# Graph attention on one core: third tile's masks ahead of the plus tables, x by rows in two halves, paired stores, and three of eight products on GpSimd

## The reference

```python
in_fts = W @ inlayer.T
f1 = (w1 @ in_fts).T + b1
f2 = (w2 @ in_fts).T + b2
logits = f1 + f2.T
bias_mat = jnp.where(adj_mat > 0, 0.0, NEG_INF).astype(logits.dtype)
coefs = jax.nn.softmax(jax.nn.leaky_relu(logits) + bias_mat, axis=-1)
vals = coefs @ inlayer
...
x = _layernorm(x + _L0_gnn_ref(x, adj, ...), axis=-1)
```

## Time and profile before

| | us |
|---|---|
| median of 3 runs | 278.81 (277.19 to 279.4) |
| profiled execution | 275.19 |
| its span | 273.5 |
| PE busy | 258.2 (94%) |
| DVE busy | 242.6 (89%) |
| ACT busy | 195.6 (72%) |
| POOL busy | 67.2 (25%) |
| PE clock granted (mean share of full speed) | 0.997 |
| DMA, mean over the span | 269 GB/s, 73.64 MB |

### The profile page before, as it was taken

One profiled execution on the slowest core, in us unless ns is written; L12 is line 12 of the kernel. 1 busy time (PEld: TensorE's weight loads), 2 busy tenths in 40 slices (PEclk: granted clock), 3 DMA queues, 4 the chain that ended last, 5 costly groups with the idle time before them and its releaser, 6 DMA issues.

```text
span 273.5 us, 5997 instructions
## 1 busy us (share of the span) xinstructions
PE 258.2 (94%) x2195; PEld 225.6 (82%) x2195; DVE 242.6 (89%) x309; ACT 195.6 (72%) x296; POOL 67.2 (25%) x98
## 2 busy tenths in 40 slices
PE   2999988799999999999999999999999999999991
PEld 2989877688888888888888888888888888888880
DVE  2888999988888899999999999999998999999963
ACT  2479999949999996999199919991999198003140
POOL 4002046930000006300630063006300630054150
PEclk9999999999999999999999999999999999999998
DMA  6999999999999999999999999999999999801011
GB/s 196 256 298 309 311 313 282 285 272 311 313 315 318 315 314 315 323 339 315 316 324 342 318 316 280 361 328 327 240 335 309 309 285 337 226 2 38 0 49 31
DMA packets 22562, 73.64 MB, mean 269 GB/s; under 512 B 3090, under 2 KB 4244, under 8 KB 22548
## 3 DMA queue, kind: packets, MB, share of 16 engines
q1 hardware_dynamic: 11184, 35.17, 42.9%
q10 hardware_dynamic: 9956, 34.64, 42.0%
q0 software_dynamic: 1408, 3.67, 4.7%
HBM read 71.37 MB, written 2.10 MB: 269 GB/s over the span
## 4 chain that ended last, share of the span: by engine, by line
DVE 58%; PE 16%; issue 8%; ACT 7%; DMA 7%; DVEq 1%; ACTq 1%; POOL 1%; POOLq 0%
DVE mn L743 19%; PE ps L1091 16%; DVE msk L756 11%; DVE mn L748 11%; DMA nat<-in_adj 5%; DVE post L855 3%; ACT sgn L474 3%; DVE ybt L870 2%; DVE bns L875 2%; ACT bt L542 2%; DVE ntot L860 2%; DVE post L857 2%; ACT post L518 2%; DMA msk<-in_x 2%; DVE mv L879 1%
## 5 line engine op out<-in xcount | busy, mean ns | idle before, releaser
L1091 PE MATMUL ps<-bt,msk 128*128 128x258 f16 x2048 | 232.1, 274 | 3.6 <-DVE msk L756 2.7
L1091 PEld LDWEIGHTS ps<-bt,msk 128*128 128x128 fp8e5 x2048 | 200.5, 98 | 34.2 <-issue 4.6
L474 ACT ACTIVATE sgn<-f2b,nf1l 128x1024 int8<-128x1024 f32 x128 | 136.4, 1144 | 5.2 <-POOL flag L409 4.0
L743 DVE TENSOR_SCALAR mn<-nat 128x4096 int8<-128x4096 int32 x32 | 73.1, 2284 | 5.0 <-DMA nat<-in_adj 4.6
L416 POOL TENSOR_SCALAR nmr<-mv 128x4 f32<-128x4 f32 x7 | 12.8, 1835 | 143.5 <-DVE mv L879 143.5
L756 DVE STREAM_TRANSPOSE msk<-mn 128x1024 uint32<-128x1024 uint32 x32 | 39.8, 1245 | 2.6
L748 DVE SCALAR_TENSOR_TENSOR mn<-sgn,mn 128x1024 uint32<-128x1024 uint32 x32 | 39.2, 1225 | 3.0 <-ACT sgn L474 2.0
L623 ACT ACTIVATE ybt<-ybt,nmr,rstd 128x128 f32<-128x128 f32 x28 | 11.5, 483 | 38.7 <-POOL nmr L421 38.7
L616 ACT ACTIVATE post<-ps,ac 128x258 f32<-128x258 f32 x60 | 24.8, 467 | 10.9 <-PE ps L1091 10.9
L761 DVE TENSOR_SCALAR msk<-msk 128x1024 uint32<-128x1024 uint32 x32 | 22.2, 695 | 1.0
L427 POOL DMA_DIRECT2D out<-ybt x24 | 13.7, 572 | 16.3 <-ACT ybt L623 14.9
(11 more groups left out here) (115 smaller groups left out, 105.2 us busy)
## 6 DMA issues: line engine op xcount, KB each, us to landing
nat<-in_adj SPq DMA_DIRECT2D x64, 512.0 KB, 15.1
nat<-in_adj ACTq DMA_DIRECT2D x64, 512.0 KB, 17.6
xn<-in_x POOLq DMA_DIRECT2D x4, 512.0 KB, 19.8
out<-ybt POOLq DMA_DIRECT2D x24, 64.0 KB, 6.6
msk<-in_x SPq DMA_DIRECT2D x8, 128.0 KB, 4.2
msk<-in_x ACTq DMA_DIRECT2D x8, 128.0 KB, 4.5
out<-ybt SPq DMA_DIRECT2D x4, 64.0 KB, 1.8
out<-post SPq DMA_DIRECT2D x4, 32.0 KB, 2.4
```

Of the source, the lines that this page charges most:

```text
L474: ins = act.activation(sgn[:, c, g * JA:(g + 1) * JA], f2b[:, :], ACT.Sign, bias=nf1l[:, bass.ds(G * t + g, 1)], scale=-1.0)
L743: dve.tensor_scalar(mn[:, c % 2], nat[:, c], 0, EDGE, ALU.is_gt, ALU.mult).then_inc(cast_done, 1)
L1091: ins = pe.matmul(ps[:, 2 * c + m, 0:2 * DV], mask_f[c][m][:, n // KB, n % KB, :], btv[m][:, n, :], start=(n == 0), stop=(n == NK - 1))
```

## The change

- VectorE: tile 2's cast, combination and transpose move ahead of the plus tables. Tile 1's cast moves ahead of the third minus `low_x`. `f2_rows` comes before the two small reductions of f2, the first `spread_f1` between the product and the reduction of the last chunk.
- TensorE: the `gram` matmuls come before the first edge sums; the minus sums of tiles 0, 1 and 2 come before any plus sums; plus tables are used in the order `ORDER = (1, 0, 2, 3)`.
- GpSimd multiplies chunks 2 and 3 of table 1 and chunk 1 of table 0 with `cs` (`scale_pool`): two before the denominators' columns, one after the second minus table is ready. The eight activations of ACT for chunk 3 of table 1 and those for chunk 1 of table 0 go, and DVE's `scale_x` of chunk 2 of table 1. The checks for `flag` are joined into fewer instructions, part of them earlier.
- ScalarE: more of f2's sums are taken by its accumulating copies (chunk 1 and chunk 2, four blocks each), `nf1l`'s first part is copied here, signs of tile 2 come before the second plus table, and tile 7's far halves are loaded right after the signs of tile 4.
- SyncE: the near halves of tiles 1 to 3 are issued after chunk 2 of x has landed.
- x by rows: two loads of 1 MB (`load_rows`), the first after `flag`, the second after `rows` of quad 1.
- Stores: two quads together, four DMAs of 128 KB in place of eight of 64 KB; tiles of the last quad are one DMA each.

```diff
+            def scale_pool(m, h):
+
+                pool.wait_ge(xl_in[h], 16 * A)
+                pool.wait_ge(cs_ready[m], 1)
+                return pool.tensor_tensor(ybuf[:, h], xl_chunk(h),
+                                          cs[:, m, h * CN:(h + 1) * CN, None].to_broadcast([P, CN, D]), ALU.mult)
+
+
+            for h in range(BCH // 2, BCH):
+                scale_pool(1, h).then_inc(y1_pool, 1)
...
+            pool.wait_ge(table_ready[1], 2)
+            scale_pool(0, 1).then_inc(y0_pool, 1)
...
+            def load_rows(h):
+
+                for g in range(G):
+                    pool.dma_start(xn[g * SQ:(g + 1) * SQ, h * NT // 2:(h + 1) * NT // 2, :],
+                                   x_h[h, g]).then_inc(xn_in, 16)
...
+                for turn in range(1, NQ // 2):
                     rows(2 * turn - 1, 1)
-                    store(2 * turn - 1, 1)
+                    if turn == 1:
+                        load_rows(1)
+                    store(turn - 1)
                     rows(2 * turn, 0)
...
-            for t in range(QT):
+            load_near(0, 0)
+
+            sp.wait_ge(xl_in[2], 16 * A)
+            for t in range(1, QT):
                 load_near(t, t)
...
             sp.wait_ge(tile_ready, 1)
-                for g in range(G // 2):
-                    store_last(sp, QT - 1, 1, g)
+                sp.dma_start(out_t[NT - 1], post[:, 1, 0, QT - 1, 0:D]).then_inc(last_stored, 16)
...
+            stat_max(1, 2, 4)
+            cast(2, 2, 0)
+            stat_out(1, 2, 4)
+            combine(2, 2)
+            dve.wait_ge(y0_pool, 1)
+            turn(2, 2)
```

More of the change, by code:

```diff
@@ L236, in gat_kernel @@
         last_stored = sem("last_stored")
-        out_stored = [sem(f"out_stored{i}") for i in range(2)]
+        out_stored = sem("out_stored")
         flag_ready = sem("flag_ready")
@@ L340, in _ @@
                         apart(sp)
[L341 to L344, removed]
+                        sp.dma_start(out_t[QT * q + c], ybt[:, 1, 0, :]).then_inc(g_stored, 16)
+                        sp.wait_ge(g_stored, 16 * (QT * q + c + 1))
                         apart(sp)
@@ L469, in load_far, with signs @@
                     load_part(act, t, c, a)
-            def signs(t, c, between=None):
+            def signs(t, c, between={}):
                 for g in range(G):
@@ L475, in signs @@
                                          bias=nf1l[:, bass.ds(G * t + g, 1)], scale=-1.0)
-                    if g == 1 and between:
-                        between()
+                    if g in between:
+                        between[g]()
                 ins.then_inc(sign_ready, 1)
@@ L560, in _ @@
             xT_out(3)
[L561 to L562 removed]
             act.wait_ge(f2b_ready, 1)
             act.wait_ge(nf1l_ready, 1)
[L565 removed]
+            signs(0, 0, between={1: lambda: xT_out(4)})
             load_far(3, 3)
             split_x(1, 0)
[L568 removed]
+            xT_out(5)
+            split_x(1, 1)
             act.wait_ge(nF2_ready, 1)
@@ L643, in _ @@
                 evacuate(0, 0, 2)
-                ahead(0, 3, 4)
+                ahead(0, 3, 4, True)
                 ahead(0, 3, 5)
@@ L674, in _ @@
                 normalise_last(1, 2, 1)
-                act.wait_ge(tile_ready, 1)
-                for g in range(G // 2, G):
-                    store_last(act, QT - 1, 1, g)
             with act.Else():
@@ L816, in _ @@
             turn(1, 1)
+            stat_max(1, 2, 4)
[4 more added lines that the diff above has]
+            turn(2, 2)
+            plus(0, 0)
+            low_x(0, 1)
+            plus(1, 1)
             dve.wait_ge(cs_ready[0], 1)
             scale_x(0, 2)
-            stat_max(1, 2, 4)
+            low_x(0, 0)
             scale_x(0, 3)
-            plus(0, 0)
-            low_x(0, 0)
-            plus(1, 1)
-            stat_out(1, 2, 4)
-            low_x(0, 1)
+            dve.wait_ge(y_act, 1)
+            plus(2, 2)
             low_x(0, 2)
             low_x(0, 3)
-            cast(2, 2, 0)
-            combine(2, 2)
-            dve.wait_ge(y_act, 2)
-            turn(2, 2)
-            plus(2, 2)
             cast(3, 3, 0)
@@ L1147, in _ @@
             edge_sums(2, 1)
-            for h in range(BCH):
-                plus_sums(h, [2])
+            pe.wait_ge(den_ready[0], 1)
+            pe.wait_ge(xeps_ready, 1)
+            plus_sums(ORDER[0], range(2))
+            plus_sums(ORDER[1], range(2))
+            plus_sums(ORDER[0], [2])
+            plus_sums(ORDER[1], [2])
+            plus_sums(ORDER[2], range(3))
+            plus_sums(ORDER[3], range(3))
             pe.wait_ge(gst_ready, 2)
@@ L1154, in _ @@
             edge_sums(3, 1)
-            for h in range(BCH):
+            for h in ORDER:
                 plus_sums(h, [3])
```

263 lines of the change are left out of this document (121 added, 142 removed).

## The result

| | before | after |
|---|---|---|
| median of 21 runs of each, in turns, us | 274.6 | 275.97 |
| lowest and highest, us | 273.77 to 279.4 | 274.96 to 281.23 |
| ratio after to before, 95% interval | | 1.005 (1.0028 to 1.0072) |
| profiled execution, us (its span) | 275.19 (273.5) | 275.71 (273.9) |
| PE busy / DVE busy / ACT busy / POOL busy | 258.2 / 242.6 / 195.6 / 67.2 | 258.6 / 246.2 / 192.7 / 71.9 |

The change makes the kernel 0.5% slower, 1.4 us. The forecast was 0.2% faster (278.2 against 278.81). The three runs on which its absolute numbers rested (277.19 to 279.4) lie above the 274.6 of the longer series, so the ratio is what can be compared. The loss is within the 1% that the forecast called the limit of what can be told, but it has the other sign, and its interval leaves out the forecast's 0.998.

A forecast was written before the change was run, and what follows sets the result against it. PE was bound by its latest start-up wait plus 0.112 us per remaining matmul. PE's end at 267.2 instead of 267.4 and a 0.4 us shorter tail gave -0.6 us: 278.2 against 278.81, range 274.0 to 282.0.

The forecast's parts named there:

- 0.4 us off the 6.07: Program's tail after PE's end: storing the last tile with one issue on SP makes it 0.4 us shorter.
- two places can be the latest wait now: PE's start-up: latest wait is the statistics transpose after 8 matmuls or tile 2's after 64; ends 267.15 or 267.2.
- Before it began at 21.99, waiting for DMA, so that earlier rows of tile 0 bring nothing here: Tile 0's cast on VectorE: put at 22.5, against 21.99 before, so earlier rows gain nothing.
- The walk: VectorE's start-up, row by row: statistics at 38.3, tile 2 transposed at 45.0, PE's end about 267.2 us.
- rival B: GpSimd's three products on VectorE's path are long: over 1% slower from 3.1 us each; 0.17 together with Rival C's bad case.
- Of the 7.3 us almost nothing is left: Tile 2's transpose: PE's wait ends 7.3 us earlier, but 64 fewer matmuls (7.2 us) are done by then.
- Rival A: VectorE doesn't wait for GpSimd's products: cast at 20.5, 274.2 us (-4.6); chance 0.35, counted with a short product.
- Rival C: Transfers hide the gain: if tile 1 is late for its cast, each us is lost; 0.17 together with rival B.
- Paired stores: GpSimd's output stores: half as many issues beside PE's stream, gain 0; VectorE's waits covered by its lead.
- the flag: Flag comes earlier, so signs of tile 4 no longer wait 4.0 us for it; hidden, no gain.

The follow-up runs named there:

- r0: The kernel before, run again with no edit: 274.72 us, ratio 1.0001, span 272.5.
- r1: The changed kernel with the last tile stored by four DMAs of 16 KB from two engines again: 275.62 us, ratio 1.0035 to the kernel before.
- r5b: The changed kernel with GpSimd's third product started only after the statistics reductions: 273.15 us, ratio 0.9947 to the kernel before.
- r6b: The changed kernel with 12 unread matmuls of 128 columns in TensorE's idle time before the f1 rows: 274.31 us, ratio 0.9988 to the kernel before.
- r4b: The changed kernel with the first 16 edge matmuls of tile 0 before gram again: 275.3 us, ratio 0.9995 to the kernel before.
- r2: The changed kernel with all three products moved from GpSimd to VectorE: 275.72 us, ratio 1.0045 to the kernel before.
- r10: The changed kernel without SyncE's wait for x's third chunk ahead of the near halves of tiles 1 to 3: 276.0 us, ratio 1.0045.
- r7b: The changed kernel with first 16 sums before gram, last tile in four DMAs, and third product behind the statistics: 275.2 us, ratio 1.0014.
- r11: r5b's kernel with GpSimd's second product also moved, beside tile 0's transpose: 274.33 us, ratio 0.9986 to the kernel before.
- r3: The kernel before with a single DMA of 64 KB for the last tile: 275.48 us, ratio 1.0019.

## Why the prediction was wrong

**The sum against the measurement.** Forecast -0.6, measured +1.4 (275.97 - 274.6). Profile to profile the change cost +0.52 (275.71 - 275.19): TensorE's end 0.0 (267.45 against 267.43, where the forecast said -0.2), the tail +0.4 (forecast -0.4), the time around the span +0.12 (1.81 for 1.69; forecast 0). The remaining 0.85 is the traces against their medians: before's was 0.59 above its 274.6, after's 0.26 below its 275.97.

The spans show where that is, without single traces: their median is 273.05 over r0's 12 runs of before and 274.1 over the changed kernel's 21, 1.05 us more. With 0.4 of it in the tail, an estimate from these numbers leaves 0.65 us up to TensorE's end, where the forecast had -0.2. So both terms of the sum had the wrong sign.

**The first failed step: "0.4 us off the 6.07", the tail.** It was worked from issue lengths alone: one issue in place of two. The traces show 3.3 us from VectorE's last instruction to the end for one DMA of 64 KB, and 2.9 us for four of 16 KB. The issue is shorter (0.53 us for 0.80); the landing is later. The term has the wrong sign and is 0.8 of the 2.0 us by which the forecast missed. In the traces this is plain; in the times it is indicated, not shown, since r1's interval overlaps.

**The second: the limits, in "two places can be the latest wait now".** The forecast named the statistics' transpose and tile 2's and missed a third: f1's spread. It is last in the changed kernel (34.44), and GpSimd's third product stands right ahead of it. The forecast charged that product 2.0 us, which was about right (1.7), to the statistics. What it put at nothing is TensorE's own work behind f1's spread: 4.06 us to the statistics' transpose at 38.50, which had been ready at 37.27. Nor did it price the pace. The reordering, with `gram` first, had taken away the 16 sums that kept TensorE busy in that place, and full speed came at 37.95 in place of 32.97. r5b (the hold away, -2.8 us), r6b (the idle time filled, -1.7) and r4b (the old order, -0.7, with intervals that all but touch) show it from three sides.

**The base.** "Before it began at 21.99, waiting for DMA, so that earlier rows of tile 0 bring nothing here" rested on one execution. In r0 the cast came at 21.01 without a wait and TensorE's end 1.0 us earlier. The walk was subtracted from a trace 0.6 us above its own median.

**Luck.** The walk's end was close to the trace's (267.2 for 267.4), but by errors that cancel: the statistics were ready 1.0 us before the forecast's 38.3, and TensorE reached them 1.2 us after they were ready.

**What was right.** VectorE waits for GpSimd's products: the forecast charged 2.0 us each and the rows show 3.0 for two and 1.7 for the third. The Trainium skill's rule cited there ("SBUF — State Buffer", section "SBUF: two separate sides"), that whichever engine starts first holds the shared ports for its whole instruction, fits the rows in both directions: VectorE's rows grow, and GpSimd's product takes 3.87 us when it starts behind a cast. It fits r5b's transpose too, which has one SBUF input and wasn't held; for the small instruction behind it, which was, no run shows why. The product itself is 1.90 us undisturbed, forecast 2.0, so rival B has no ground (its 3 x 1.1 - 0.6 is 2.7, not 2.8). Tile 2 was turned at 44.67 (forecast 45.0), the statistics stood at 37.3 (38.3), the pace was 0.112. "Of the 7.3 us almost nothing is left", because fewer matmuls are done at the earlier wait, is what happened. Rival A was false in its condition; r2 shows its cast time and why it would not have paid as worked out: adj lands at 20.8, and TensorE idles before f1 all the same. Rival C: r10 finds nothing, and tile 1's cast didn't wait in the changed kernel, but it waited 1.49 us for adj in r7b and 0.45 in r11. Paired stores cost a hidden 1.19 us of VectorE's wait at 153.52, the flag came at 44.65 and the 4.0 us of the earlier trace rows went, hidden too.

**What stays open.** Why the time around the span grew by 0.12 to 0.15 us: its median is 1.83 over 21 runs of the changed kernel and 1.69 over 12 of r0. It is 1.70 in r3 and 1.83 to 1.86 in r1 and r2, so it lies neither with the last store nor with GpSimd's products. GpSimd's and VectorE's loop code changed, but no run takes that apart. Why one 64 KB DMA lands later than four of 16 KB is measured and not explained.

## What to carry to other kernels

Moving element-wise work to GpSimd isn't free help for VectorE: put such an instruction beside VectorE work that takes no second input (a transpose), never ahead of the one that TensorE waits for; one wait on GpSimd turned this change from 0.5% slower to 0.5% faster. When a reordering lets TensorE idle before it has reached full speed, count the work behind at half pace for longer, and fill the gap with useful matmuls if they can stand there. And compare a forecast's base with more than one execution when the wait it rests on ends with a DMA.

## What the runs showed that was not expected

- A VectorE instruction held by GpSimd shows no idle time, but a longer duration: 2.92 us for 1.22, and 5.40 for 2.41.
- TensorE ran its first sums at 0.215 us and later ones at 0.112, while the windows' clock column read 1.00; the trace's own record of the clock begins only with full speed, at 37.95 us. Twelve unread matmuls in an idle gap made the program 1.7 us faster.
- The stretch behind such a gap varied by 1.3 us between kernels with the same code there (7.25, 7.31, 8.26, 8.58 us), which is as much as the change's effect.
- One DMA of 64 KB over 128 partitions ended the program 3.3 us after its data was ready, four of 16 KB on two queues 2.9 us.
